# Taking batches up one tile sooner in the second mixture of a two-layer macaron block

## The reference, cut to what matters

```python
x = x + 0.5 * _L0_ffn_ref(_layernorm(x), ...)      # first mixture: 8 experts, top 2
x = x + _L0_attn_ref(_layernorm(x), ...)
x = x + 0.5 * _L0_ffn_ref(_layernorm(x), ...)      # second mixture: same experts
x = x + 0.5 * _L1_ffn_ref(_layernorm(x), ...)      # third: 16 experts, top 2, capacity 640
x = x + _L1_attn_ref(_layernorm(x), ...)
x = x + 0.5 * _L1_ffn_ref(_layernorm(x), ...)      # fourth
```

## Time and profile before

| | us |
|---|---|
| median of 3 runs | 1414.9 (1414.76 to 1420.95) |
| the profiled execution, its own time | 1410.61 |
| its span, first to last instruction | 1408.6 |
| start of the second mixture's first scatter and of its last send, on POOL | 722.77 and 933.36 |
| first transpose of the third mixture on PE | 938.25 |

### The profile page before, as it was taken

The page is one execution under the profiler, slowest core; times in us unless marked ns, Lnnn a source line. Parts: engine busy times, 40 slices in busy tenths (PEclk is TensorE's granted clock), DMA queues, the critical chain, the costliest instruction groups (busy, mean ns, idle before and its releaser), DMA issues.

```text
span 1408.6 us, 25294 instructions
## 1 busy us (share of the span) xinstructions
PE 1169.6 (83%) x7427; PEld 783.6 (56%) x7427; DVE 849.5 (60%) x2809; ACT 733.2 (52%) x1579; POOL 701.1 (50%) x940
## 2 busy tenths in 40 slices
PE   4399897899999999999689998239999767389994
PEld 3299885122223232232279987227899656268894
DVE  7534666888898999988432665702126787421235
ACT  4155543577767767767545554214446566234441
POOL 3777443213233454524764477745554277625543
PEclk9999998799999999999979999559999987589997
DMA  9687767435435435251357886425577041145586
GB/s 306 174 227 217 207 187 226 152 103 159 141 97 156 132 88 147 69 145 36 121 151 234 258 234 183 134 75 171 167 218 238 26 136 37 48 142 175 173 267 195
DMA packets 171541, 223.69 MB, mean 159 GB/s; under 512 B 24000, under 2 KB 125888, under 8 KB 171408
## 3 DMA queue, kind: packets, MB, share of 16 engines
q1 hardware_dynamic: 133168, 174.67, 43.2%
q0 software_dynamic: 18080, 37.20, 7.7%
q10 hardware_dynamic: 20160, 10.23, 2.6%
HBM read 150.55 MB, written 71.21 MB: 157 GB/s over the span
## 4 chain that ended last, share of the span: by engine, by line
PE 54%; DVE 17%; POOL 9%; DMA 6%; issue 6%; ACT 5%; SPq 3%; DVEq 0%; ACTq 0%; POOLq 0%
PE PS L1510 17%; PE PS L1520 16%; POOL dispatched L830 6%; DVE arena L2435 6%; PE PS L1698 5%; PE PS L1674 5%; PE PS L1488 2%; ACT arena L1223 2%; PE PS L1682 2%; PE PS L1660 2%; DMA arena<-experts 2%; DVE X L1982 1%; DMA qk_products<-arena 1%; DVE BST L1972 1%; DVE arena L2084 1%
## 5 line engine op out<-in xcount | busy, mean ns | idle before, releaser
L1094 ACT ACTIVATE arena<-PS,arena 128x128 f32<-128x128 f32 (+2 forms) x696 | 280.0, 451 | 347.7 <-PE PS L1510 338.0
L852 POOL DMA_INDIRECT expert_out<-arena x309 | 297.7, 963 | 289.7 <-issue 173.7
L1223 ACT ACTIVATE arena<-PS 128x512 f32<-128x512 f32 x512 | 283.8, 596 | 133.5 <-PE PS L1674 132.5
L2435 DVE TENSOR_REDUCE arena<-PS 128x2 f32<-128x1024 f32 x256 | 300.9, 1216 | 25.6 <-PE PS L1684 24.7
L1510 PE MATMUL PS<-arena 128*128 128x128 f32 (+2 forms) x1392 | 309.4, 366 | 4.5 <-issue 1.1
L1520 PE MATMUL PS<-arena 128*128 128x128 f32 (+1 forms) x2472 | 307.1, 276 | 3.7 <-DVE arena L2244 3.5
L1520 PEld LDWEIGHTS PS<-arena 128*128 128x128 f32 x2472 | 298.6, 192 | 17.4 <-issue 5.9
L2244 DVE TENSOR_TENSOR arena<-PS,arena 128x128 f32<-128x128 f32 (+2 forms) x174 | 68.6, 394 | 328.4 <-PE PS L1520 324.9
L1510 PEld LDWEIGHTS PS<-arena 128*128 128x128 f32 x1392 | 221.8, 194 | 46.4 <-issue 7.3
L830 POOL DMA_INDIRECT dispatched<-arena x192 | 185.3, 965 | 82.3 <-issue 57.9
L1674 PE MATMUL PS<-arena 96*128 96x512 bf16 x512 | 173.6, 390 | 11.2 <-ACT arena L1223 5.4
(11 more groups left out here) (273 smaller groups left out, 1180.0 us busy)
## 6 DMA issues: line engine op xcount, KB each, us to landing
arena<-experts SPq DMA_DIRECT2D x103, 578.0 KB
qk_products<-arena SPq DMA_DIRECT2D x48, 384.0 KB, 4.4
arena<-qk_products SPq DMA_DIRECT2D x64, 288.0 KB
arena<-experts SPq DMA_DIRECT2D x71, 256.0 KB
dispatched<-FILL SPq DMA_DIRECT2D x32, 322.5 KB, 6.7
YC<-expert_out SPq DMA_DIRECT2D x36, 256.0 KB
arena<-dispatched SPq DMA_DIRECT2D x71, 129.0 KB
arena<-qk_products SPq DMA_DIRECT2D x64, 128.0 KB
```

The costliest lines, as they stand in the source:

```text
L852: pool.indirect_dma_start(YK, bass.IndirectOffsetOnAxis(ap=ID[:, s:s + 1], axis=0), YS[:, s, :], None).then_inc(s_yo[r], 16)
L1094: act.activation(bent(f, tau)[:, q, 0:N], bank(q, 0, N), func, bias=bias).then_inc(s_g, 1)
L1223: act.activation(PT[:, G % 2, j, k, :], bank(4 + k % 2), ACT.Exp, scale=float(1.0 / np.sqrt(HD))).then_inc(s_exp, 1)
L2435: dve.tensor_reduce(MX[:, G % 2, head:4:2, a], PS[:, 1024 * w:1024 * w + 1024].rearrange("p (a b) -> p a b", a=2), AX_X, ALU.max).then_inc ...
```

## The change

S moves one step sooner for batches 0 to 5, and each later step of a batch's routing stands one step nearer to S. `moments` and `inverse_deviation` move from step S+1 to the end of step S, behind the second half of the combination.

| batch | 0 | 1 | 2 | 3 | 4 | 5 | 6 | 7 |
|---|---|---|---|---|---|---|---|---|
| S before | 17 | 19 | 23 | 27 | 31 | 35 | 40 | 42 |
| S after | 16 | 18 | 22 | 26 | 30 | 34 | 40 | 42 |
| placed before | 22 | 24 | 28 | 32 | 36 | 40 | 45 | 47 |
| placed after | 20 | 22 | 26 | 30 | 34 | 38 | 44 | 46 |

```diff
             if carries(L):
-                return max(tiles_to(L, b) + 4, early_tiles(L) + E0 + 3 + 2 * b)
+                return max(tiles_to(L, b) + 3, early_tiles(L) + E0 + 2 + 2 * b)
...
         def place_of(L, b):
-            return start_of(L, b) + 5
+            return start_of(L, b) + 4
...
                     if carries(L):
+                        for b in starting(L, c - 1):
+                            scale_rows(b, NG)
                         for b in starting(L, c - 2):
-                            scale_rows(b, NG)
-                        for b in starting(L, c - 3):
                             carried_rows(b)
                             second_rows(b, NG)
...
-                        for b in starting(L, c - 4):
+                        for b in starting(L, c - 3):
                             carried_logits(b)
...
-                        for b in starting(L, c - 5):
+                        for b in starting(L, c - 4):
                             carried_ranks(b)
-                        for b in starting(L, c - 3):
+                        for b in starting(L, c - 2):
                             carried_turn(b)
...
-                        for b in starting(L, c - 4):
+                        for b in starting(L, c - 3):
                             scores_in(b, E1, bank(5, 0, GT * E1), n + b)
                         for b in starting(L, c):
                             gather(f, b, 0)
-                        for b in starting(L, c - 1):
-                            moments(b)
...
-                        for b in starting(L, c - 1):
-                            inverse_deviation(b)
-                        for b in starting(L, c - 4):
+                        for b in starting(L, c - 3):
                             chosen_out(b, E1, n + b)
...
                         for b in starting(L, c):
                             gather(f, b, 1)
+                            moments(b)
+                            inverse_deviation(b)
```

## The result

| | before | after |
|---|---|---|
| median of the runs | 1414.83 us (6 runs, 1411.78 to 1420.95) | 1445.51 us (6 runs, 1442.10 to 1449.48) |
| profiled execution, own time | 1410.61 us | 1442.88 us |
| first scatter of tile 14 to last send | 157.4 us | 182.2 us |

By the medians the changed kernel is slower by 30.7 us; the ratio of the runs is 1.0205, with a 95% interval of 1.0185 to 1.0225. The forecast was 1433.7 us, in the range 1419 to 1445. The direction and the mechanism were right, but the size was 12 us short, and the median lies half a microsecond above the upper end of the range.

A forecast was written before the change was run, and what follows sets the result against it. POOL's gapless transfers bound the kernel from tile 22; a circle of waits, less saved sends, adds 15.4 us and the clock 3.4: +18.8, 1410.6 to 1429.4. With the median 4.3 above: 1433.7 us, range 1419 to 1445.

The forecast's parts named there:

- What bounds the kernel before: Second mixture: from tile 22 on POOL's transfers are the bound; PE catches up only at the very end.
- The train: POOL's scatters and sends without gaps from tile 22 to the last send, about 1.267 us per transfer.
- The sends: POOL's left-over sends at the mixture's end: starting two tiles sooner leaves 34 instead of 38, -5.1 us.
- The block: DVE's combination half, moments, inverse deviation and placement before a tile's copy: 5.70 us; PE waits about 3 us per batch.
- only the block costs: Rival: landings precede ACT's request, POOL bounds from tile 20; tile 38 7.1 us late, less 5.1: +2 us; chance 0.09.
- The landing: Second scatter's start until ACT can load `YC`: taken as 3.37 us; PE waits for it through `XT`.
- the circle: Waits through PE, DVE, POOL's scatters, landing, ACT's load and `XT`, once per four tiles: 22.6 us a round against POOL's 20.3.
- the head: Start of the stretch, tile 14 to tile 20: delayed by first block and landing; tile 20's first scatter near 811.
- The clock: PE slowed after idle waits of some 3 us: +3.4 us, in the start and behind the last block, none in rounds.
- Tile 20 to tile 38: Part of the mixture where the circle's rounds of 22.6 us replace POOL's 20.3 us per four tiles.
- Everything at its upper bound: Rival: four landings of 4.55 us (+4.7) and clock loss every round (+5.2): +28.7, 1443.6 us; chance 0.15.

The follow-up runs named there:

- the second execution: Changed kernel profiled again with no edit: stretch (first scatter of tile 14 to last send) 190.8 us, +33.5; ratio 1.0209.
- the load alone: Kernel before with only ACT's load of `YC` asked one step sooner: stretch 168.4 us, +11.0; ratio 1.0106.
- the block alone: Kernel before with moments and inverse deviation moved into the combination's step, start and routing steps unchanged: stretch 171.0 us, +13.6; ratio 1.0112.

## Why the prediction was right, and where its size was off

- **What bounds the kernel before: right.** The train came out the same to 0.1 us in a second execution, and taking PE's 2.50 us away gained nothing.
- **The sends: right.** 34 remain, the tail is 5.1 us shorter, in both executions of the changed kernel.
- **The block: right in length** (from its second half of the combination at 847.93 to the copy at 853.73 it is 5.80 us, forecast 5.70) and in the wait (3.0 us five times, 1.23 us once, forecast six times 3). By itself it costs 13.6 us, though, and not the 7.1 us that the rival "only the block" had ahead of its saved sends: the rival's round of PE stays below POOL's only while the clock holds.
- **The landing: mechanism right, the price too low.** The prediction took 3.37 us. The eight landings that stood in the circle in the two executions of the changed kernel were 4.17 to 5.31 us, 4.55 on average, which is the upper bound that the prediction had kept for the range. The 4.2 us of the first execution's rounds against 3.37 explain its 23.5 us against 22.6, and the 4.62 of tile 18 about 1.3 us of the head. By the fit in the Trainium skill's "DMA: Bandwidth & Descriptors" (Anatomy of one DMA) the prediction had an estimate of 3.1 us for it; the measurements are above both. The same page of the Trainium skill has the rule to issue a transfer early and to wait for it late (Rules for kernel authors). The runs agree with it: with the load one step later and nothing that PE needs behind it, the same sooner start cost 0.8 us of the stretch instead of 25.4.
- **The clock: the step that failed in kind.** The prediction counted +3.4 us, half in the start and half behind the last block, and none in the rounds, because "a loss behind the block shortens PE's wait for the load". That holds for the block's wait, as the first execution shows. It does not hold for the wait for the landing itself, behind which the prediction counted nothing in the rounds: behind 4.59 us of it the router product took 1.89 us instead of 0.96 and L1510 3.68 instead of 1.89, which is +2.7 us, and nothing later absorbed it. In the second execution this happened in every round. The head, forecast at +10.6 us up to tile 20 (12.3 with the 1.7 us of clock that the sum has in the start), was +16.4: 3.5 us more than the 10.6 until batch 1's router product (1.3 of landing, some 1.2 of half clock behind the wait at 791.00, the rest small), and 2.3 more behind it, mostly that clock loss.
- **Tile 20 to tile 38:** forecast +9.8 us by the circle; +13.4 and +22.9 measured. With landings of 4.2 us instead of 3.37 and no loss of clock, three rounds add 2.5 us to the forecast; the second execution's further 9.4 are longer landings and half-clock rows.
- **The terms together.** The first execution's +24.8 us are 6.0 above the forecast of +18.8: four landings above 3.37 us make 4.3 of it, and the half-clock rows behind the waits at 791.00 and 812.49 come to 4.1 where 3.4 had been counted (behind the last block nothing was lost, L1510 taking 1.89 us at 901.58). The second execution's +33.5 are 14.7 above: 5.2 from the landings, and 8.6 from the clock, some 10 us behind the four waits for `XT` and 1.8 behind the last block against the 3.4. About 1 us is left over in each. So the landing, priced too short, is most of the miss in the one execution, and the clock in the other. In the first, tile 38's first scatter came at 917.91 (forecast near 908) and the third mixture's first transpose at 967.23 (near 957), of which 4.1 us each are the later tile 14.
- **"Everything at its upper bound"** (+28.7 us) was the rival that came nearest to the +30.7 of the medians, and its two terms are the two that were too small, though it laid the clock's loss to the block. In the second execution the rows behind the four waits for `XT` are 2.9, 1.9, 3.6 and 1.9 us longer than the same rows at full clock, together 10 of the 33.5 us. The Trainium skill's "TensorE: Matmul & The Clock Gate" (What's actually happening) puts the cost of warming up below 1% of a typical kernel's span and advises not to fit a count of cold products. The trace agrees with the share, 10 us being 0.7% of that execution's 1446.6 us; for the price of a change of 2% such a share is not small.

The two parts do not simply add: the load alone costs 11.0, the block alone 13.6, and less the 5.1 of saved sends their sum is 19.5, below the 24.8 and 33.5 of the two executions. What stays open is why the clock fell behind one 3 us wait and not behind another (847.53 and 867.57 above), and why the landings were longer than 3.37 us; no run here controls either, so the cost in the stretch can be given only by its two measured executions, 25 and 34 us.

## What to carry to other kernels

Before a wait is moved nearer to the transfer that it waits for, look at what stands behind it on the same queue: here a load's wait for a landing cost 11 to 25 us where rows that PE needs stood behind it, and about nothing where they stood ahead of it and the load came a step later. Compare an engine's round, waits included, with the round of the engine that bounds: a wait of 3 us was hidden while PE's round was 20.0 us against POOL's 20.3, and left gaps in POOL's train once a lost clock made the round 22.9. And do not price a landing by a single row: read every landing of that transfer in the stretch and use the long ones when it comes to stand on a chain of waits.

## What was not expected of the hardware

Waits of nearly the same length (3.22 us at 847.53, 3.35 us at 867.57, in the same kernel) left PE at full clock in one case and at half clock in the other (granted clock 1.00 and 0.50), with 1.91 and 3.62 us for the same eight-instruction product. And the stretch of the kernel before, where POOL's train sets most of it, was the same to 0.1 us in two executions, while that of the changed kernel, a circle of waits, differed by 8.7 us. Two executions of each do not make a rule, but a circle of waits should not be priced from one.
